# Keeping x on chip, a fourth echo bank, and column 2 used ahead of its turn, in a two-layer graph kernel

## The reference

```python
def _L0_gnn_ref(x, adj, u):
    keep = (u >= 0.1).astype(x.dtype)
    return jnp.matmul(adj, x * keep / 0.9)
def _L1_gnn_ref(x, adj, weight, bias):
    return jnp.matmul(adj, jnp.matmul(x, weight)) + bias
h = _layernorm(x + _L0_gnn_ref(x, adj, u))
y = _layernorm(h + _L1_gnn_ref(h, adj, weight, bias))
```

## Time and profile before

| | |
|---|---|
| median of three runs | 898.15 us |
| the profiled execution | 898.45 us |
| its span, first to last instruction | 896.5 us |
| PE busy | 863.1 us, 96% |
| DVE busy | 560.9 us, 63% |
| ScalarE (ACT) busy | 21.3 us |
| moved by DMA | 359.73 MB |

### The profile page before, as it was taken

One profiled execution on the slowest core, in us unless ns is written; L12 is line 12 of the kernel. 1 busy time (PEld: TensorE's weight loads), 2 busy tenths in 40 slices (PEclk: granted clock), 3 DMA queues, 4 the chain that ended last, 5 costly groups with the idle time before them and its releaser, 6 DMA issues.

```text
span 896.5 us, 15757 instructions
## 1 busy us (share of the span) xinstructions
PE 863.1 (96%) x6790; PEld 482.7 (54%) x6790; DVE 560.9 (63%) x1144; ACT 21.3 (2%) x59; POOL 25.3 (3%) x24
## 2 busy tenths in 40 slices
PE   3899999999999999999999999999999999999996
PEld 2664554445767546555555564646545566456432
DVE  6356123145155757775777777778777777867755
ACT  0100000000000000000000000000000000000011
POOL 3000000000000000000000000000000000000133
PEclk9999999999999999999999999999999999999998
DMA  9999999999999999999999999999999999999962
GB/s 373 412 416 420 421 419 420 421 420 421 420 420 420 419 421 419 421 400 402 420 421 406 423 419 397 419 372 422 372 410 421 415 423 419 420 423 419 420 256 71
DMA packets 55412, 359.73 MB, mean 401 GB/s; under 512 B 6448, under 2 KB 10544, under 8 KB 12592
## 3 DMA queue, kind: packets, MB, share of 16 engines
q1 hardware_dynamic: 55344, 358.74, 96.9%
HBM read 356.61 MB, written 2.10 MB: 400 GB/s over the span
## 4 chain that ended last, share of the span: by engine, by line
PE 85%; DMA 7%; DVE 4%; SPq 2%; issue 2%; ACT 0%; POOLq 0%; POOL 0%; DVEq 0%
PE psum L1033 20%; PE psum L986 19%; PE psum L967 8%; PE psum L1001 8%; PE psum L995 8%; PE psum L1019 6%; DMA tiles<-adj_chunks 5%; PE psum L953 5%; PE psum L974 4%; PE psum L1039 4%; DMA tiles<-adj_t 2%; PE psum L930 1%; SPq L500 1%; DVE layer L654 1%; DVE layer L709 1%
## 5 line engine op out<-in xcount | busy, mean ns | idle before, releaser
L986 PE MATMUL psum<-tiles,stat 128*64 128x256 f32 x1952 | 218.3, 379 | 1.6 <-DMA tiles<-adj_t 1.6
L1033 PE MATMUL psum<-tiles,stat 128*64 128x512 f32 x944 | 210.3, 593 | 0.6 <-issue 0.3
L654 DVE TENSOR_TENSOR layer<-psum,layer 128x512 f32<-128x512 f32 (+1 forms) x143 | 98.7, 690 | 154.6 <-PE psum L1033 58.0
L986 PEld LDWEIGHTS psum<-tiles,stat 128*64 128x64 f32 x1952 | 147.1, 137 | 72.4 <-issue 7.5
L1033 PEld LDWEIGHTS psum<-tiles,stat 128*64 128x64 f32 x944 | 69.2, 137 | 119.8 <-issue 115.8
L690 DVE TENSOR_TENSOR tiles<-tiles 128x512 f32<-128x512 f32 x90 | 62.2, 691 | 53.8 <-PE psum L976 52.2
L1003 PE MATMUL psum<-tiles,stat 128*64 128x256 f32 x360 | 92.6, 380 | 0.0
L969 PE MATMUL psum<-tiles,stat 128*64 128x256 f32 x360 | 92.4, 379 | 0.0
L967 PE MATMUL psum<-tiles,stat 128*64 128x256 f32 x360 | 92.4, 379 | 0.0
L967 PEld LDWEIGHTS psum<-tiles,stat 128*64 128x64 f32 x360 | 49.3, 137 | 37.8 <-issue 16.7
L678 DVE TENSOR_TENSOR tiles<-tiles 128x512 f32<-128x512 f32 x90 | 60.6, 684 | 8.0 <-DMA tiles<-adj_t 8.0
(11 more groups left out here) (100 smaller groups left out, 852.5 us busy)
## 6 DMA issues: line engine op xcount, KB each, us to landing
tiles<-adj_t SPq DMA_DIRECT2D x306, 1024.0 KB, 13.6
tiles<-adj SPq DMA_DIRECT2D x12, 1024.0 KB, 19.2
tiles<-adj_chunks SPq DMA_DIRECT2D x12, 1024.0 KB, 20.4
tiles<-xu SPq DMA_DIRECT2D x4, 1024.0 KB, 8.0
tiles<-adj_parts SPq DMA_DIRECT2D x16, 256.0 KB, 17.6
x_res<-x SPq DMA_DIRECT2D x16, 128.0 KB, 14.4
out<-layer SPq DMA_DIRECT2D x8, 256.0 KB, 2.2
w<-weight SPq DMA_DIRECT2D x4, 16.0 KB, 10.2
```

Of the source, the lines that this page charges most:

```text
L654: return dve.tensor_tensor(out=to, in0=addend, in1=to, op=ALU.add)
L986: last = pe.matmul(sum_f[i % 2][to, left], stat[:, j * C + c, 0:D], tile[:, c, columns], start=begun.get("f") != i and c == 0, stop=ends a ...
L1033: last = pe.matmul(bank[to, :], stat[:, j * C + c, D:2 * D], tile[:, c], start=c == 0, stop=c == C - 1)
```

## The change

Three things are edited, and the order of work follows from two of them.

1. x is no longer loaded a second time. ACT copies x out of the four staged loads into the right half of `stat`, where h of the same block is written later, and signals `x_kept`. `turn` and `turn_part` read x there. The 16 transfers into `x_res`, their waits and the buffer go. `h_bias` moves to `layer1`. SP waits for `x_kept` as well before a slot of the staged loads is used again.
2. `turned` moves to the right halves of the two banks of `sum_f`, which frees bank 4, and `ECHO_BANKS` is 4. PE's waits before it begins a new sum in a bank of `sum_f` are on `turned_read` (the turn has been read) in place of the copies' counters. The planner puts the pieces left over from the opening behind two filler jobs (`JOINS_LAST = 2`) and no longer behind three.
3. `MORE_FROM = (12,)`: for rows 12 to 15 tiles of column 2 go to `early` jobs, E12,2 and E14,2, which come into the list once h of block 2 is known, and `fused` begins at column 3 in these rows. Four `fused` jobs go, two `early` jobs come.

```diff
+MORE_FROM = (12,)
-ECHO_BANKS = 3
+ECHO_BANKS = 4
+JOINS_LAST = 2
 def begins_at(i):
-    return EARLY if i >= EARLY else 0
+    return EARLY + sum(i >= row for row in MORE_FROM) if i >= EARLY else 0
 def has_fused(i):
-    return i > EARLY
+    return i >= EARLY and i > begins_at(i)
...
-            if pieces and (len(filler) == ECHO_BANKS if i > 1 else len(filler) % 2 == 0):
+            if pieces and (len(filler) == JOINS_LAST if i > 1 else len(filler) % 2 == 0):
...
+        if EARLY <= i - 1 < EARLY + len(MORE_FROM):
+            early = sorted(early + [("early", r, i - 1) for r in range(MORE_FROM[i - 1 - EARLY], NB, 2)], key=lambda job: job[1:])
...
-        x_res = sb("x_res", [P, 2, C * D])
...
-        h_bias = [x_res[:, :, :].rearrange("p n (c d) -> p (n c) d", d=D),
-                  halves[:, :].rearrange("p (c d) -> p c d", d=D)]
+        h_bias = [layer1[:, n].rearrange("p (c d) -> p c d", d=D) for n in (1, 2)]
...
-        turned = banks[4]
-        echo = banks[5:8]
+        turned = [bank[:, B // 2:B] for bank in sum_f]
+        echo = banks[4:8]
...
-                if rows_begun == 0 and part == 1 or rows_begun >= 1 and kind in ("first", "fused") and tile[0] == rows_begun:
-                    i = rows_begun
-                    if i >= 2:
-                        sp.wait_ge(turned_read, turns(i - 2))
-                    sp.dma_start(x_res[:, i % 2], x_v[:, i]).then_inc(s_res[i % 2], 16)
-                    rows_begun += 1
                 if new and staged <= slot:
                     sp.wait_ge(dropped, XU)
+                    sp.wait_ge(x_kept, XU)
...
+            for g in range(XU):
+                act.wait_ge(s_xu[g], 16)
+                act.activation(rows_of_x(g, slice(D, 2 * D)), xu_stage[:, g, :, 0], ACT.Copy).then_inc(x_kept, 1)
...
-                dve.wait_ge(s_res[i % 2], 16 * (i // 2 + 1))
                 dve.wait_ge(h_ready, k)
-                last = dve.transpose(turned[:, 0:B // 2], source[:, 0:B // 2])
+                last = dve.transpose(turned[i % 2], source[:, 0:B // 2])
...
-                x_rows = x_res[:, i % 2].rearrange("p (c d) -> p c d", c=C)
+                x_rows = stat[:, i * C:(i + 1) * C, D:2 * D]
...
                         if begun.get("f") != i:
-                            if i <= 2:
-                                pe.wait_ge(half_by_act, turns(i - 2))
-                            pe.wait_ge(half_by_dve, turns(i - 2))
+                            pe.wait_ge(turned_read, turns(i - 2))
```

More of the change, by code:

```diff
@@ L294, in place_tiles, with resnorm_graph_layers @@
     return loads, place
-def resnorm_graph_layers(nc: bass.Bass, x, xu, adj_t, adj_parts, adj_0, adj_chunks, weight, bias, out):
+def resnorm_graph_layers(nc: bass.Bass, xu, adj_t, adj_parts, adj_0, adj_chunks, weight, bias, out):
     jobs = order_of_work()
@@ L334, in resnorm_graph_layers @@
     complete = {i: max(n for n, row in enumerate(joined) if row in (i, i + 1)) + 1 for i in range(0, NB, 2)}
-    x_v = x.rearrange("(b p c) d -> p b (c d)", p=P, c=C)
     out_v = out.rearrange("(b p c) d -> p b (c d)", p=P, c=C)
@@ L405, in resnorm_graph_layers, with rows_of_x @@
             "p s (b n k d) -> p s b n k d", b=PARTS, n=2, d=D)
+        def rows_of_x(g, half):
+            return stat[:, g * PARTS * C:(g + 1) * PARTS * C, half].rearrange("p (b k) d -> p b k d", b=PARTS)
         psum = ctx.enter_context(nc.psum_tensor("psum", [P, 8, B], F32))
@@ L434, in resnorm_graph_layers @@
         s_xu = [sem(f"xu_loaded_{n}") for n in range(XU)]
-        s_res = [sem(f"x_res_loaded_{n}") for n in range(2)]
         s_small = sem("weight_bias_loaded")
@@ L439, in resnorm_graph_layers @@
         dropped = sem("x_dropped")
+        x_kept = sem("x_kept")
         zeroed = sem("sums_zeroed")
@@ L474, in _ @@
                 sp.dma_start(tiles[:, staged + g], xu[g]).then_inc(s_xu[g], 16)
-            rows_begun = 0
             for n, (tile, part, slot, freed, new, kind) in enumerate(loads):
@@ L633, in _ @@
                 dve.scalar_tensor_tensor(
-                    out=stat[:, t, 0:D].rearrange("p (b k) d -> p b k d", b=PARTS), in0=xu_stage[:, g, :, 1], scalar=DROP,
+                    out=rows_of_x(g, slice(0, D)), in0=xu_stage[:, g, :, 1], scalar=DROP,
                     in1=xu_stage[:, g, :, 0], op0=ALU.is_ge, op1=ALU.mult).then_inc(dropped, 1)
@@ L741, in turn_part @@
                 rows = r[:, q:q + 1, :]
-                t = turned[:, :].rearrange("p (c f) -> p c f", c=C)[:, q:q + 1]
-                dve.wait_ge(s_res[0], 16)
+                t = turned[part_bank(q)][:, 0:P].unsqueeze(1)
+                dve.wait_ge(x_kept, XU)
                 if q:
@@ L747, in turn_part @@
                 step(dve.scalar_tensor_tensor(out=rows, in0=t[:, :, 0:D], scalar=KEPT,
-                                              in1=x_res[:, 0].rearrange("p (c d) -> p c d", c=C)[:, q:q + 1],
+                                              in1=stat[:, q:q + 1, D:2 * D],
                                               op0=ALU.mult, op1=ALU.add))
@@ L767, in turn @@
                     step(last)
-                t = turned[:, 0:B // 2].rearrange("p (c e f) -> p c e f", c=C, f=QUAD)
-                x_rows = x_res[:, i % 2].rearrange("p (c d) -> p c d", c=C)
+                t = turned[i % 2].rearrange("p (c e f) -> p c e f", c=C, f=QUAD)
+                x_rows = stat[:, i * C:(i + 1) * C, D:2 * D]
                 for side in range(2):
@@ L910, in _ @@
                     if g == 0 and q >= 2:
-                        pe.wait_ge(half_by_act, q - 1)
-                        pe.wait_ge(half_by_dve, q - 1)
+                        pe.wait_ge(turned_read, q - 1)
                     if g == 0 and q:
@@ L941, in _ @@
                     pe.wait_ge(half_by_dve, q + 1)
-                    pe.transpose(turned[:, of_part(q)], halves[:, of_part(q)], ident[:, :]).then_inc(turned_ready, 1)
+                    pe.transpose(turned[part_bank(q)][:, 0:P], halves[:, of_part(q)], ident[:, :]).then_inc(turned_ready, 1)
                 elif kind in ("chunk", "rest"):
@@ L1054, in _ @@
                     else:
-                        pe.wait_ge(half_by_dve, turns(NB - 1))
+                        pe.wait_ge(turned_read, turns(NB - 1))
                         pe.wait_ge(combined, 2 * combined_rows(NB - 1))
@@ L1086 @@
     arrays = {
-        "x": np.ascontiguousarray(x),
         "xu": np.ascontiguousarray(xu).reshape(XU, P, C, B),
```

## The result

The changed kernel takes 892.38 us (median of four runs, 892.28 to 892.60) against 898.15 beside it: a ratio of 0.9935, 95% interval 0.9923 to 0.9948. That is 5.8 us less; 892.7 was forecast. The profiled execution took 892.40 us with a span of 890.6.

What follows compares the result with a forecast made beforehand. PE's work and the tile loads were both nearly full, PE alone deciding behind the last tile wait. Terms -2.9 - 1.7 - 0.5 - 1.9 + 1.65 = -5.4 us gave 892.7 us, 8-in-10 range 890.8 to 895.2.

Steps and rivals of the forecast that it cites:

- What bounds the kernel: Whole run: PE's work and tile loads both nearly full; behind the last wait for a tile, PE's work alone counts.
- E10,1 at 191.1: Row 2's new order and x off the stream: this landing-set start comes 2.9 us earlier, bounds 2.0 to 4.0.
- The bytes of a transfer: Load stream: each 128 KB transfer of x takes 0.31 us; three count ahead of E10,1, 0.93 us.
- F6,15 at 333.4 with 1.4 us of reserve: Row 6's filler: PE could start at 333.4, tile lands at 332.0, so 1.7 us of waiting goes.
- P2,7 at 451.0: The late `pair`: PE starts at 451.0, its tile lands at 449.5, so 0.5 us of waiting goes.
- rival C: Landings before 191 us come earlier still: 4.0 us gained at E10,1, no other wait, 891.6 us; 12%.
- rival D: Landings fall on `first` jobs of rows 4 to 9, waits return, relief half undone: 895.4 us; 9%.
- 1.65 us more work from two `early` for four `fused`: Column 2: 13.74 us of PE's work added, 12.1 us removed in rows 12 to 15, all on the path.
- The fourth bank, 1.9 us: Joins behind rows 14 and 15: waits of 1.5 us at s11,14 and 0.4 us at P8,14 go.
- Rival B: Behind row 14: h takes the bank's place, the 1.9 us stay, 894.6 us; 15% with A's mild form.
- ACT's copies: Opening: four copies of x at 1.26 us each, over 10 us of cover before first use, no cost.
- Rival A, the slots: Rows 3 to 6: late loads break the stream; 894.6 us mild, 901.2 at worst; slower in the end 4%.

Runs made afterwards that it cites:

- E12,2: Not a run: an `early` job of PE on column 2 tiles, added by the change in row 3; 6.87 us of PE's work.
- E14,2: Not a run: the second `early` job of PE on column 2 tiles, added by the change in row 3; 6.87 us.
- banks alone: Kernel before with only the fourth echo bank and `turned` in the banks of `sum_f`, old order of jobs: 896.08 us against 898.22.
- E8,1: Not a run: an `early` job of PE, at 187.07 us in the kernel before; 8.58 us in place of 6.87 with the banks alone.
- x alone: Kernel before with only x copied from the staged loads and its 16 transfers gone; three echo banks, old order: 894.86 us against 898.22.
- the order undone: Changed kernel with the opening's pieces back behind three filler jobs (`JOINS_LAST = 3`): 894.25 us, 1.9 more than the changed kernel.
- column 2 alone: Kernel before with only E12,2 and E14,2 added and four `fused` jobs less: 897.53 us against 898.22, ratio 0.9994.
- Column 2 undone: Changed kernel with `MORE_FROM` empty, so all rows begin `fused` at column 2: 892.88 us, 0.5 more than the changed kernel.

## Why the prediction was right, point by point

*What bounds the kernel* held. PE starts on a landing up to E10,1 and never behind it. The banks alone show what that means. Their profile has E10,1 at 195.9, 1.9 us later than before, though its tile was there at 192.17: the lower clock behind E8,1 had made PE late. Yet F6,15 starts at 324.3 as before. Its tile landed at 324.22, and PE, with no idle time now, was only just ready for it. The lost 1.9 us had gone into the waits of row 6, and P2,7 started on its landing (442.16) at 442.25. So in a kernel that still has these waits, a loss of their size ahead of them costs nothing at the end.

*E10,1 at 191.1*: measured 190.95. That it came out to 0.15 us is in part luck. With x alone E10,1 starts at 192.6, 1.3 us before its old place, where the forecast had 0.93; the order undone moves it by 1.6 us, where the forecast leaves 2.0. The two misses cancel. The bytes of a transfer at 420 GB/s make 0.31 us; 0.37 and 0.36 were measured at F6,15. That is the term that was mis-sized, by a sixth, and it explains 1.1 of the 1.3 us; the rest is no more than the landing of this tile varies between profiles with the same loads ahead of it (191.83, 191.96 and 192.17 in those of column 2 alone, before and the banks alone). In the sum the term counts only three times, which is why it did little harm; x alone, where seven to nine transfers count, came out 0.7 us under its forecast.

*F6,15 at 333.4 with 1.4 us of reserve*: measured 333.1 with the tile at 331.51, 1.6 us of reserve; nothing waits. Column 2 undone brings back the wait with a start at 321.60 (321.6 forecast) and costs 0.5 us (0.6 forecast). *P2,7 at 451.0*: measured 450.8, its tile at 449.02 (449.5 forecast). Neither rival C (4.0 us at E10,1) nor rival D (waits in other places) happened.

*1.65 us more work from two `early` for four `fused`*: not seen by itself, but the whole balance closes on it. From P2,7 to s11,14 the distance to before goes from +8.3 to -2.4 us; three of the four `fused` (9.1) and the bank's wait (1.5) make 10.6 of these 10.8.

*The fourth bank, 1.9 us*: 2.1 alone and 2.2 undone, of which 0.2 and 0.3 us stand already at the last start that a landing sets, so about 1.9 both times. Its thin place also stood as worked out: h(14) is written by 779.06 (778.58 and 0.48), s11,14 starts at 779.37, and the join of P2,13, the first of the three from 780.08 on, ends at about 780.8 (a third of 2.28 us), before P12,14 asks for it at 781.09. Rival B did not happen, with 0.3 us to spare.

*ACT's copies*: 1.06 us each (1.26 was taken), the last done at 14.3 us, 12 us before their first reader, DVE at 26.34. The turn's sums from `stat` kept their 287 ns.

*Rival A, the slots*, did not happen with 17 slots: the least time from issue to landing there was 7.6 us, more than the 6.3 forecast. With fewer slots it was right in its mechanism and wrong in its place. I looked for the least reserve in rows 3 to 6 because loads were added there. With 15 slots they cost the most at the starts of rows 8 to 13, where held tiles and `pair` jobs stand in a row. With 17 slots PE has enough in hand there to bridge a broken stream (0.97 of the DMA engines' time between 540 and 600 us, before in the earlier trace rows and in the changed kernel); with 15 it has not.

The parts don't add up to the whole: x 3.4, banks 2.1 and column 2 0.7 make 6.2 alone, and the order adds its own, against 5.8 together. x and column 2 remove the same waits in rows 6 and 9: x alone leaves 0.44 us of them, column 2 alone none.

## What to carry to other kernels

Where two streams are both nearly full, find the last start that a landing sets: ahead of it the bytes of the loads count and the engine's work hardly at all, behind it only the engine's work, and one job's start on either side gives the sum. An edit that buys less waiting with more work (column 2, 2.2 us for 1.65) is worth its balance only, and less once other edits have removed the same waits. Ask for the reserve of a shared resource along the whole run, not only where the edit is made.

## What the runs showed of the hardware that was not expected

A transfer of 128 KB in a full queue between 1 MB transfers took 0.36 to 0.37 us of the stream (seven fewer: 2.59 us; 21 more: 7.6 us), 0.05 us more than its bytes at the stream's 420 GB/s. One wait of 2.05 us and four of 2.8 to 4.2 us of TensorE came with stretches of 3.5 to 7.5 us at a granted clock of 0.53 to 0.62, but not every wait of that length did: behind 1.89 us in the same place in the kernel before, and behind 2.25 us at 92.53 in the changed kernel, it stayed at 1.00. The time around the span is not constant either: with spans within 0.3 us of each other (890.0 to 890.3), five runs of one kernel measured from 891.9 to 893.1 us.
